# A step's waits laid out anew, and closing keys that GpSimd reads half from the key rows in four pieces

## The reference

```python
xn = _layernorm(x, axis=-1)
x = x + _L0_gnn_ref(xn, W, b, edge_index) + _L0_mix_ref(xn[None], Wq, bq, Wk, bk, Wv, bv, Wo, bo)[0]
x = x + _L0_ffn_ref(_layernorm(x, axis=-1)[None], ...)[0]

# in _L0_ffn_ref, for every expert, head and token in turn (E, TOPK, H, DK, DV = 4, 2, 8, 64, 64):
q = _l2norm(_silu(h @ Wq)); k = _l2norm(_silu(h @ Wk)); v = _silu(h @ Wv)
beta_e = beta[None] * m[..., None]          # m: the token is routed to this expert
g_e = jnp.where(m[..., None], g[None], 0.0)
def step(S, x):
    qt, kt, vt, bt, gt = x
    S = S * jnp.exp(gt)[..., None, None]
    kv = jnp.einsum('bhk,ebhkv->ebhv', kt, S)
    delta = (vt[None] - kv) * bt[..., None]
    S = S + kt[None, :, :, :, None] * delta[..., None, :]
    ot = jnp.einsum('bhk,ebhkv->ebhv', qt * scale, S)
    return (S, ot)
```

## Time and profile before

| | |
|---|---|
| device time, median of 3 | 869.64 us (866.48 to 873.55) |
| the profiled execution: device time | 871.51 us |
| the profiled execution: span on the core | 869.7 us |
| TensorE: matmul busy | 795.5 us (91%), 10074 matmuls |
| TensorE: weight loads busy | 532.2 us (61%) |
| VectorE busy | 639.5 us (74%) |
| ScalarE busy | 312.0 us (36%) |
| GpSimd busy | 291.5 us (34%) |
| mean granted TensorE clock | 0.984 |

### The profile page before, as it was taken

One profiled execution on the slowest core, in us unless ns is written; L12 is line 12 of the kernel. 1 busy time (PEld: TensorE's weight loads), 2 busy tenths in 40 slices (PEclk: granted clock), 3 DMA queues, 4 the chain that ended last, 5 costly groups with the idle time before them and its releaser, 6 DMA issues.

```text
span 869.7 us, 23569 instructions
## 1 busy us (share of the span) xinstructions
PE 795.5 (91%) x10074; PEld 532.2 (61%) x10074; DVE 639.5 (74%) x1345; ACT 312.0 (36%) x547; POOL 291.5 (34%) x280
## 2 busy tenths in 40 slices
PE   2998999999999999999999986999998999997698
PEld 1454444444566667865444446888888888897343
DVE  6999999995888856535843647887787878783385
ACT  1231112210122230023654533656555555653342
POOL 5221110000111141000673335656655565561650
PEclk9998999999999999999999997999999999999899
DMA  8600000023000016000049643454545455521452
GB/s 244 200 0 1 0 2 1 0 49 72 1 1 0 2 47 221 0 1 1 5 132 394 263 119 101 131 133 133 164 122 142 126 137 144 133 65 40 128 174 71
DMA packets 74961, 80.46 MB, mean 93 GB/s; under 512 B 34453, under 2 KB 57671, under 8 KB 74854
## 3 DMA queue, kind: packets, MB, share of 16 engines
q1 hardware_dynamic: 69733, 57.78, 24.0%
q0 software_dynamic: 5120, 21.14, 6.7%
HBM read 54.44 MB, written 24.39 MB: 91 GB/s over the span
## 4 chain that ended last, share of the span: by engine, by line
PE 69%; DVE 23%; issue 4%; POOL 1%; ACT 1%; DMA 1%; SPq 1%; DVEq 0%; POOLq 0%; ACTq 0%
PE bank L786 14%; PE bank L869 8%; PE bank L894 4%; PE bank L1069 4%; PE bank L582 4%; DVE rows L1558 3%; PE bank L596 3%; DVE rows L1687 3%; DVE rows L1560 3%; PE bank L801 2%; PE bank L885 2%; PE bank L994 2%; PE bank L919 2%; PE bank L798 2%; PE bank L956 2%
## 5 line engine op out<-in xcount | busy, mean ns | idle before, releaser
L786 PE MATMUL bank<-W,xT 128*128 128x512 f32 x280 | 124.2, 596 | 0.7 <-ACT big L1148 0.7
L786 PEld LDWEIGHTS bank<-W,xT 128*128 128x128 f32 x280 | 52.0, 190 | 60.2 <-issue 58.4
L560 PE MATMUL bank<-W,xT 128*125 128x512 f32 x160 | 79.2, 609 | 0.0
L1387 POOL TENSOR_TENSOR cnt_r<-cnt_r,ident_sb 125x125 fp32r<-125x125 f32 x10 | 11.4, 1144 | 173.8 <-ACT cnt_r L1134 173.8
L582 PEld LDWEIGHTS bank<-rows 128*126 128x126 f16 x360 | 43.5, 135 | 34.7 <-issue 24.2
L1693 DVE TENSOR_SCALAR rows<-iota_sb,tC 128x625 f16<-128x625 f16 x180 | 56.2, 378 | 10.5 <-PE bank L582 10.5
L582 PE MATMUL bank<-rows 128*126 128x313 f16 x360 | 58.9, 299 | 4.2 <-DVE rows L1693 4.1
L1558 DVE TENSOR_SCALAR rows<-iota_sb,gbp 125x180 f16<-125x180 f16 x160 | 56.2, 351 | 0.0
L1560 DVE TENSOR_SCALAR rows<-iota_sb,gbp 125x180 f16<-125x180 f16 x160 | 50.3, 315 | 0.0
L570 PE MATMUL bank<-rows 125*128 125x360 f16 x160 | 42.7, 321 | 5.1 <-DVE rows L1560 3.3
L1236 ACT ACTIVATE tB<-bank 128x1024 f16<-128x1024 f32 x40 | 40.9, 1024 | 13.8 <-PE bank L919 6.9
(11 more groups left out here) (336 smaller groups left out, 1916.8 us busy)
## 6 DMA issues: line engine op xcount, KB each, us to landing
big<-qkv_slots SPq DMA_DIRECT2D x40, 256.0 KB, 3.6
rows<-step_rows SPq DMA_DIRECT2D x40, 128.0 KB, 3.1
rows<-gam_rows SPq DMA_DIRECT2D x40, 128.0 KB, 3.5
big<-qkv_slots SPq DMA_DIRECT2D x80, 64.0 KB, 2.7
big<-qkv_slots SPq DMA_DIRECT2D x40, 128.0 KB, 3.0
o_slots<-big SPq DMA_DIRECT2D x40, 128.0 KB, 2.9
x_all<-in_x SPq DMA_DIRECT2D x10, 224.0 KB
out<-tC SPq DMA_DIRECT2D x10, 224.0 KB
```

Source lines behind the costliest of these rows:

```text
L560: last = mm(dst, xT[:, k, t * P:(t + 1) * P], W[:, w, k, :], start=(k == 0), stop=(k == KC - 1 and bias is None))
L786: last = mm(bank[:, b0, :], xT[:, k, t * P:t * P + 128], W[:, w, k, :], start=(k == 0), stop=(k == KC - 1))
```

## The change

Waits. The semaphores `b_done` and `tm_done` become one, `level_ready`, which both producers raise, so a level waits once for twice the count; the mask that only VectorE and ScalarE look at gets `b_masked`. TensorE drops second waits that other waits imply: `ati_done` in `residual` (ScalarE's `keep_t` waits for it now), `tt_done` in `first_fix` and `kg_done` in `old_keys` (kept, as `kd_done`, in the last two units), `tf_done` in `solve`, `kd_done` in `state_part`, `qg_done` in `out_part`. ScalarE drops one in `key_features` and two a step in `keep_z`, and in `keep_t` the wait for `tf_done` moves behind the first copy. VectorE drops `pt_done` before the scan, `tt_psum` in `pairs`, and `o_psum` in `new_state`.

Keys. `closing_keys` is four instructions of 64 partitions x 256 elements, each behind a wait for the one before. The two whose head half and chunk agree (b = c) read the key rows in `qkn`, the other two read `kp`, of which only these halves are still loaded: two 64 KB copies a step in place of four. The key rows of unit h + 2 overwrite those that `closing_keys(h)` now reads, so `load_qk(h + 2, 1)` moves behind `load_vp(h)` in SyncE's queue and behind a wait for `kd_done`.

The diff, without the list of semaphore names and most unchanged lines:

```diff
-        def b_count(u, lv):
...
-            return (2 * LEVELS - FLIP - 1) * u + lv + max(lv - FLIP + 1, 0)
+        def masked_count(u, lv):
...
+            return (LEVELS - FLIP) * u + lv - FLIP + 1
         def feature_count(t, w):
...
             def load_kp(u, c):
...
-                    for b in range(2):
-                        sp.dma_start(kp[u % 2][CL * b:CL * b + CL, c * HB:(c + 1) * HB, :], per[u, b][:, c]).then_inc(kp_loaded[u % 2], 16)
+                    b = 1 - c
+                    sp.dma_start(kp[u % 2][CL * b:CL * b + CL, c * HB:(c + 1) * HB, :], per[u, b][:, c]).then_inc(kp_loaded[u % 2], 16)
             def load_vp(u):
...
                     if h >= 1:
...
-                    load_qk(h + 2, 1)
                 if h >= 3:
                     store_o(h - 3)
                 if h + 2 < NSC:
...
                     load_vp(h)
                 if h + 2 < NSC:
+                    sp.wait_ge(S["kd_done"], h + 1)
+                    load_qk(h + 2, 1)
...
             def level_up(u, lv):
...
-                pe.wait_ge(S["b_done"], b_count(u, lv))
-                pe.wait_ge(S["tm_done"], level_count(u, lv))
+                pe.wait_ge(S["level_ready"], 2 * level_count(u, lv))
...
             def last_level(u):
...
-                pe.wait_ge(S["b_done"], b_count(u, lv))
-                pe.wait_ge(S["tm_done"], level_count(u, lv))
+                pe.wait_ge(S["level_ready"], 2 * level_count(u, lv))
...
             def residual(u):
...
-                pe.wait_ge(S["ati_done"], u + 1)
...
             def first_fix(u):
...
-                pe.wait_ge(S["tt_done"], u + 1)
+                if u + 2 >= NSC:
+                    pe.wait_ge(S["tt_done"], u + 1)
...
             def old_keys(c):
...
-                if c2 == 0:
-                    pe.wait_ge(S["kg_done"], u + 1)
+                if c2 == 0 and u + 2 >= NSC:
+                    pe.wait_ge(S["kd_done"], u + 1)
...
             def solve(c):
...
-                if c2 == 0:
-                    pe.wait_ge(S["tf_done"], u + 1)
...
             def state_part(c):
...
-                if c2 == 0:
-                    pe.wait_ge(S["kd_done"], u + 1)
...
             def out_part(c):
...
-                if c2 == 0:
-                    pe.wait_ge(S["qg_done"], u + 1)
...
-                    act.wait_ge(S["kg_done"], u - 1)
-                    act.wait_ge(S["qg_done"], u - 1)
+                    act.wait_ge(S["kd_done"], u - 1)
                 A(kF[s], bank[:, TB[s], :].rearrange("p (a n) -> p a n", n=CL), ACT.Copy).then_inc(S["kF_done"], 1)
             def query_features(u):
...
             def keep_mt(u):
...
-                A(MT16[s], bank[:, TB[s], :].rearrange("p (a n) -> p a n", n=CL), ACT.Copy).then_inc(S["tm_done"], 1)
+                A(MT16[s], bank[:, TB[s], :].rearrange("p (a n) -> p a n", n=CL), ACT.Copy).then_inc(S["level_ready"], 1)
             def keep_tm(u, lv):
...
-                    act.wait_ge(S["b_done"], b_count(u, lv + 1) - 1)
+                    act.wait_ge(S["b_masked"], masked_count(u, lv + 1))
...
                     A(TT16[s].rearrange("p (z a) n -> p z a n", z=2),
-                      bank[:, TB[s]:TTB[s] + 1, :].rearrange("p z (a w n) -> p z a w n", w=2, n=CL)[:, :, :, 0, :], ACT.Copy).then_inc(S["tm_done"], 1)
+                      bank[:, TB[s]:TTB[s] + 1, :].rearrange("p z (a w n) -> p z a w n", w=2, n=CL)[:, :, :, 0, :], ACT.Copy).then_inc(S["level_ready"], 1)
...
-                    A(TM[s].rearrange("p (z a) w n -> p z (a w n)", z=2), bank[:, TB[s]:TTB[s] + 1, :], ACT.Copy).then_inc(S["tm_done"], 1)
+                    A(TM[s].rearrange("p (z a) w n -> p z (a w n)", z=2), bank[:, TB[s]:TTB[s] + 1, :], ACT.Copy).then_inc(S["level_ready"], 1)
             def keep_t(u):
...
+                act.wait_ge(S["ati_done"], u + 1)
...
+                A(flat(T0), bank[:, TB[s], :], ACT.Copy).then_inc(S["t_done"], 1)
...
-                A(flat(T0), bank[:, TB[s], :], ACT.Copy).then_inc(S["t_done"], 1)
...
                 A(flat(TT), bank[:, TTB[s], :], ACT.Copy).then_inc(S["tt_done"], 1)
...
             def keep_z(c):
...
-                if c >= 2:
-                    act.wait_ge(S["o_psum"], c - 1)
                 A(flat(zt[c % 2]), bank[:, DA, HW2:2 * HW2], ACT.Copy).then_inc(S["z_done"], 1)
             def keep_o(c):
...
             def closing_keys(u):
...
-                pool.wait_ge(kp_loaded[u % 2], 64 * (u // 2 + 1))
+                pool.wait_ge(kp_loaded[u % 2], 32 * (u // 2 + 1))
...
-                G.tensor_tensor(kD[p][s], kp[s], bc(bdec[:, 2 * u:2 * u + 2, :].rearrange("p c j -> p (c j)"), CL), ALU.mult).then_inc(S["kd_done"], 1)
+                pool.wait_ge(S["qg_done"], u + 1)
+                for n, (b, c) in enumerate(((0, 0), (1, 1), (0, 1), (1, 0))):
+                    q, a = slice(CL * b, CL * b + CL), slice(c * HB, (c + 1) * HB)
+                    own = qkn[s][q, D:2 * D].rearrange("p (j b n) -> p j b n", b=2, n=DH)[:, :, b, :]
+                    if n:
+                        pool.wait_ge(S["kd_part"], 3 * u + n)
+                    G.tensor_tensor(kD[p][s][q, a, :], own if b == c else kp[s][q, a, :], bc(bdec[q, 2 * u + c, :], CL),
+                                    ALU.mult).then_inc(S["kd_part" if n < 3 else "kd_done"], 1)
+                pool.wait_ge(S["kd_done"], u + 1)
             def unit_of(stage, u, *lv):
...
-                if u >= 2:
-                    dve.wait_ge(S["pt_done"], u - 1)
                 V.tensor_tensor_scan(flat(EB[s]), flat(arow[s]), flat(EBS[s]), 0.0, ALU.mult, ALU.add).then_inc(S["eb_done"], 1)
             def pk(s, w):
...
             def pairs(u):
...
-                if u >= 2:
-                    dve.wait_ge(S["tt_psum"], u - 1)
...
                 V.transpose(B16[0][s], TT16[s]).then_inc(S["t16_done"], 1)
...
-                    V.tensor_tensor(B16[lv % 2][s], pm(MB[s]), bm(level[lv], 8), ALU.mult).then_inc(S["b_done"], 1)
+                    V.tensor_tensor(B16[lv % 2][s], pm(MB[s]), bm(level[lv], 8), ALU.mult).then_inc(S["level_ready"], 1)
...
                     V.tensor_tensor(by_bank(flipped), pk(s, 1), level[lv].unsqueeze(1).unsqueeze(1).broadcast_to([128, 2, HB, CL]),
-                                    ALU.mult).then_inc(S["b_done"], 1)
-                    dve.wait_ge(S["b_done"], b_count(u, lv) - 1)
-                    V.transpose(B16[lv % 2][s], flipped).then_inc(S["b_done"], 1)
+                                    ALU.mult).then_inc(S["b_masked"], 1)
+                    dve.wait_ge(S["b_masked"], masked_count(u, lv))
+                    V.transpose(B16[lv % 2][s], flipped).then_inc(S["level_ready"], 1)
             def residual(u):
...
             def new_state(c):
...
-                if c:
-                    dve.wait_ge(S["o_psum"], c)
                 V.tensor_tensor(state[:, (c + 1) % 2, :, :], pd(0), sdec[:, :, :], ALU.add).then_inc(S["state_done"], 1)
             def unit_of(stage, u, *lv):
```

4 lines of the change are left out of this document (2 added, 2 removed).

## The result

The changed kernel takes 856.72 us (median of 6 runs, 854.66 to 859.71), the kernel before 869.83 us beside it (6 runs, 866.48 to 873.55): a ratio of 0.9847, 95% interval 0.9814 to 0.9881. It is 13 us faster where 2.8 were forecast, and 0.3 us under the low end of the range.

What follows compares the result with a forecast made beforehand. TensorE was taken as the bound, stopping where a 256-instruction packet ends and the next isn't there. -3.3 - 1.3 + 1.8 = -2.8 us, taken off the 869.64 median: 866.8, said as 867; range 857 to 876.

Steps and rivals of the forecast that it cites:

- Much of what shortens work inside a stretch is lost in the idle time: TensorE between packet ends: stretches take 4.15 to 4.62 us whatever their work; only removing instructions is gained in full.
- The prediction's own sign for it: In the loop: 10 us shorter would prove that the waits, not the fetches, set the pace.
- Term 1: TensorE's list: 196 second waits dropped, 0.77 of an instruction packet at about 4.3 us; -3.3 us (0 to -12).
- None of the waits dropped is late today: TensorE's dropped waits: all are already met when reached, so no stall moves elsewhere; no cost added.
- Term 2: DMA in the loop: two `kp` copies a step fewer, less load slowing TensorE's instruction fetches; -1.3 us (0 to -2.5).
- Term 3: GpSimd's closing keys in four pieces, 2.74 us for 1.04, delaying VectorE's scan; +1.8 us (0 to +12).
- its cover: GpSimd after the closing keys: L1427 waits 37.0 us in 19 times for the scan, so longer pieces are free there.
- the second rival: VectorE's scan is held by all four GpSimd pieces: +7.4 us, slower, 877; chance 0.2.
- L1427 still ending its idle time on the scan: Expected profile sign on GpSimd: the instruction after the four pieces still waits for VectorE's scan.
- the prediction's chain behind the scan: After VectorE's scan: L1984, then L1236, then TensorE's level 3 follow; half of 5.4 us delay exposed.
- At nothing: Moved key rows (4.4 us to spare before `features`), ScalarE's and VectorE's dropped waits, `keep_t`'s added wait: no effect.
- Waits cost their full time: TensorE's list is dispatch-bound between float16 stages; 196 waits give back 0.06 us each, 12 us: 857; chance 0.2.

Runs made afterwards that it cites:

- that row of kernels: Kernels with new waits but no key part (TensorE's only, or all engines'), plus ten long-met waits a step behind the stages' own: 0.9971, 0.9954, 0.9955; mean 0.9960.
- the met waits: Ten waits a step on a long-met semaphore, added on TensorE behind the stages' own; in the changed kernel 0.9892 and 0.9899 (859.75 and 862.71 us).
- the late wait alone: Changed kernel plus ten long-met waits a step on TensorE, written ahead of the stages' own, so the later semaphore's wait is a separate instruction: 0.9979, 867.54 us.

## Why the prediction was wrong

**What bounds the kernel: right, with one conclusion too many.** TensorE does stop at the ends of packets of 256, and the gain came from there. "Much of what shortens work inside a stretch is lost in the idle time" was taken to hold for waits too. It didn't: the idle time itself shrank, from 22.7 to 11.0 us in 18 steps (to 17.6 in the second profile). The prediction's own sign for it came, a loop shorter by 10 us, though not quite with the meaning that it gave to it: waits and fetches are no alternatives here, since the gain was made in the idle times that the fetches cause. The Trainium skill ("Runtime: NRT & Kernel Launch", section "Instruction fetch mechanics") says that the fetch is hidden behind the issue of instructions. Here it is only partly so: of the idle times of 0.4 us or more, 24 at "issue" before, 9 and 17 in the two profiles after.

**Term 1 (-3.3): the term that was mis-sized.** The step that failed is "196/256 = 0.77 of a packet, and a packet costs about 4.3 us". It counts an instruction that goes at its share of a packet, 0.017 us. Taken out while none of them was late they brought 9 us, 0.047 each, without the key part (0.02 each beside it). (The traces have 194 fewer, not 196, which changes nothing.) The second step that failed is "None of the waits dropped is late today, so no stall moves elsewhere". The premise holds, the waits dropped were the early ones; but which wait is dropped decides how the one that is left is carried. The late one, until then an instruction of its own, now rides on the weight load, and that alone is worth 0.40% (1 - 0.9960), 3.5 us, in that row of kernels, 5 us in the kernel before (0.9942) and 7 to 8 in the changed kernel. The parts do not simply add; the split depends on the kernel it is measured in. Their sum is 11 to 13 us on each path, at the upper bound of the term's range (0 to -12).

**Term 2 (-1.3): neither shown nor refuted.** Two copies more cost 1.2 us beside the changed kernel by the ratios (0.9865 to 0.9851, within both intervals) and nothing by the medians; the term is smaller than what these runs can tell. The traffic of the loop fell as said. Before, then after:

```profile
DMA packets 48493, 35.51 MB, mean 122 GB/s; under 512 B 24730, under 2 KB 43674, under 8 KB 48418
```

```profile
DMA packets 37659, 33.38 MB, mean 114 GB/s; under 512 B 13436, under 2 KB 32892, under 8 KB 37583
```

11,294 small packets fewer in the same stretch, where "some 10,000" were forecast. The share of the loop is 0.44 where 0.42 was expected; more steps now lie in the 292 us.

**Term 3 (+1.8): the cost didn't come, though its cover went.** The pieces and the scan of after (ns: shortest, median, longest):

```profile
L1457 POOL TENSOR_TENSOR W<-big,bdec x80: 604/612/1630, 517.7 to 767.7; 64x256 f32<-64x256 f32 x80
...
L1941 DVE TENSOR_TENSOR_SCAN xn<-rows x20: 1217/1402/1625, 496.1 to 754.1; 128x512 f32<-128x512 f32 x20
```

The scan of before, for comparison:

```profile
L1944 DVE TENSOR_TENSOR_SCAN xn<-rows x20: 1215/1218/1571, 497.4 to 769.5; 128x512 f32<-128x512 f32 x20
```

A piece alone takes 612 ns, as reckoned. The scan is longer by 0.18 us in the median, by 0.15 in the mean (1.39 against 1.24 us; 1.45 and 1.40 in the second profile and with the pieces alone) and by 0.4 at most. That is the delay by the one piece that is running, and the delay by all four did not happen. Two slips stand in the prediction's working: by its own rule, with the 0.12 us taken off, the mean delay over the 17 steps is 0.19 us, not 0.27, which fits better still; and its upper end of 14 us less a third is 9, not 12, so the second rival would have read 874. The contention that I took from L1961 is there in both directions: 18 of the 80 pieces, about one a step, take 1.4 us or more, up to 1.63, 1.0 more than alone. The Trainium skill ("GPSIMD Engine Reference", section "Specifications") has the interfaces shared when VectorE reads two SBUF operands; the trace agrees. What I left out is GpSimd's side of it. One step of after, GpSimd:

```profile
622.48 3.47 POOL L1457 TENSOR_TENSOR W<-big,bdec 64x256 f32<-64x256 f32 x4
626.03 1.27 POOL L1418 TENSOR_TENSOR rows<-xn,masks_sb 128x512 f32<-128x512 f32 x1
```

and VectorE in the same step:

```profile
623.36 1.49 DVE L1941 TENSOR_TENSOR_SCAN xn<-rows 128x512 f32<-128x512 f32 x1
```

Four pieces take 3.47 us, not 2.74, and end 1.1 us after the scan (623.36 + 1.49 = 624.85), so that the next instruction follows them at once. "L1427 still ending its idle time on the scan" was wrong; after, in the whole loop:

```profile
POOL rows L1418 <- DVE xn L1941: 1.3, 1, 1.3
...
POOL big L1424 <- DVE state L2003: 19.2, 12, 4.8
```

Of the 37.0 us of cover 1.3 are left, and `old_state` (L1424) waits for the state 12 times for 19.2 us where it was 20 times for 34.4. That it costs nothing in the kernel before is shown by the run with the pieces alone: 0.9998, within 2 us of none. The half of the scan's delay that I took as exposed was too much for that. Beside the rest of the key part it isn't shown, and there the prediction's chain behind the scan is real: in each of the nine profiles that have both the pieces and the new place of the key rows, the chain of waits from 560 to 760 us leads through the scan, the mask and the copy behind it (L1941, L1979 and L1228 in the changed kernel), for 6.2 and 11.3% of the stretch in the changed kernel's two and 1.6 to 8.1% in the others; in none of the eleven others, the one with the pieces alone included. No run has the copies or the new place of the key rows without the pieces, so a cost of the key part and a gain of it may cancel there.

**At nothing: right.** After, the key rows are issued ahead of `grow`, and `features` reads them 8.3 us later:

```profile
638.48 0.43 SPq L484 DMA_DIRECT2D big<-qkv_slots  x1
...
646.77 0.86 PEld L886 LDWEIGHTS bank<-ident_sb,big 128*128 128x128 f32 x8
```

VectorE's and ScalarE's waits were rightly priced at nothing: with them put back, 0.984 and 0.9855.

**The rivals.** "Waits cost their full time: 857" was right in its time and half right in its mechanism: an extra wait does cost its own time, 0.02 to 0.047 us of the 0.06 that it named, and the rest is the late wait that stood alone. That its time was right to 0.3 us is in part luck: its sum holds a term 2 at its end (-2.5) and term 3 (+1.8), of which no run shows either, and which nearly cancel. What spoke against it, stretches that last as long as the fetch, is still so after (4.54 and 4.55 us for 4.24 and 3.54 us of work); it says that a fetch that came too late isn't shortened, not that fetches go on coming too late as often. The range missed by 0.3 us because its low end was that rival's time with term 3 at +1.8, which came out near nothing.

**What stays open.** The key part is worth nothing that can be told where TensorE's list is short (0.9849 against 0.9856), but where the met waits are in the list it seems worth 5 to 6 us (0.9896 against 0.9960, with intervals that hardly touch; on one chip 862.71 against 867.71 and 867.59 us), and with the late wait alone 2 us (0.9979). Why, these runs don't tell. And the way from a separate wait to a later packet is argued only; so is the split of the gain by number, with which the ends of the packets moved.

## What to carry to other kernels

Look in the list of an engine's instructions, not only in the source, at which of a stage's waits became an instruction of its own, and write the one that comes last in time where it rides on the work; where one producer can wait on behalf of the consumer, drop the second wait. Price a wait that goes from an engine that is the bound by a run with met waits in its place, not by its share of the list: on this TensorE it was worth from a little more to almost three times that, and with it goes the order of the waits that are left. On an engine that mostly waits for others, don't expect either to be seen.

## What the runs showed of the hardware

- TensorE's idle times at "issue" stand at the ends of packets of 256 instructions: 27 of 27 at the same place of the count before, 12 of 13 after. One ends 2.4 to 2.6 us (mean) after its packet starts.
- A wait that is never late, as an instruction of its own, cost TensorE 0.02 to 0.047 us each in this list of short matmuls (0.9849 to 0.9896, and 0.9856 to 0.9960, for 194 of them).
- Which of two waits stands alone is worth 5 to 8 us for 200 waits, at the same number of instructions (0.9942, and 0.9979 against 0.9892 and 0.9899). With the late one alone, 71 and 75 of some 167 separate waits were held up by their semaphore; with a met one alone, none.
- A 64x256 product on GpSimd takes 612 ns, like a 128x256 one; caught by a two-operand scan of VectorE it takes up to 1630 ns, and the scan up to 1625 ns instead of 1218.
